# Second attention: sixteen slots for exponentials and another order of scores, products and maxima

## The chip, the core and the metric

The kernel runs on one core of one Trainium2 chip. The metric is the device time of one execution in microseconds (us), the median of the runs shown. TensorE is called PE, VectorE DVE, ScalarE ACT, GpSimd POOL and SyncE SP.

## The reference

Four batches of 1024 tokens of width 128 go through two layers, each of an attention and a feed-forward part, all with residuals and layer norms. Layer 0 is a causal attention with 16 heads of size 8 and then eight experts, of which each token takes two. Layer 1 is the attention that this change touches, and a feed-forward part with sines. Of the attention of layer 1, on `x_norm = rms_norm(x, g)`:

```python
q = (x_norm @ w_q).reshape(b, n, N_HEADS, D_HEAD)...   # 16 heads of 8
k = (x_norm @ w_k).reshape(b, n, KV_HEADS, D_HEAD)...  # 4 heads of keys and values
q = q * rf
k = k * rf
q5 = q.reshape(b, reps, KV_HEADS, n, D_HEAD)
qkt = jnp.einsum('brkqa,bkca->brkqc', q5, k) / scale
attn = jax.nn.softmax(qkt, axis=-1)                    # over all 1024 keys, no mask
s = jnp.einsum('brkqc,bkca->brkqa', attn, v)
o = s @ w_o
return s + o
```

## The kernel before

The program runs in stages that all engines pass in turn: projection and attention of layer 0 (with the routing of the experts laid between), the experts, projection of layer 1, attention of layer 1, feed-forward of layer 1. Semaphores tie the engines; each engine works through its own list in order.

An attention is done in **units**, one for a quad of four heads of one batch, 16 in all (`g` from 0). The softmax subtracts each row's maximum, so the scores are formed twice. In a unit of the second attention these are the steps; the letters are those of the string that gives their order:

- **a** (`pass_a`, L799, 32 in a unit): scores of 128 queries against all 1024 keys, two matmuls of 512 columns into one of two double banks of PSUM (banks 0 and 1, banks 2 and 3). DVE reduces them to the row maximum (L1481, 128x1024). A step a waits for the reduction of the a two before it. The a of unit g work for later units: a0 to a23 for heads 1 to 3 of unit g+1, a24 to a31 for head 0 of unit g+2. After a23's reduction DVE splits the 32 negated maxima into three bf16 parts (`negmax_split`, L1490 to L1494).
- **b** (`pass_b`, L832, 64 in a unit): transposed scores, 128 keys by 512 queries, with the maxima already subtracted through three more rows of the contraction; one matmul into one of three banks (4, 5, 7). It waits for the exponential of the b three before it, whose bank it takes. ACT then forms the exponential (L1221, 128x512) into a slot of `probs`.
- **p** (`pv`, L848, 16 in a unit): the product of four exponentials (the four heads j = 0 to 3 of one group m of 128 keys and half of the queries) with the values. Its four matmuls write 9 rows each at partitions 0, 32, 64 and 96 of bank 6; the data are float32, and the trace has two records for each matmul, eight for a p. The p of group m waits for the exponentials 4m to 4m+3. p0 to p7 make the first half of the queries, p8 to p15 the second.
- **c** (ACT, L1225): copy of a finished half out of bank 6, which the next half's first p waits for. **t** (`out_turn`, L864): four transposes of it into a bank that a step a would use. **n** (DVE, L1501 and L1506): division by the sums into `attn`.
- **m** (`negmax_turn`, L857): transpose of the split maxima of the next unit into a borrowed bank, and **s** (ACT, L1205) its copy, from which SP's DMA brings the maxima into Q for the next unit's b.

`c0` and `c1` and the like belong to the two halves. A t or m borrows the double bank of the step a that comes next, and that a waits for its reader (n or s); an m that uses the bank of a t waits for that t's n.

`ORDERS[1]` is the string. `Heads.order` turns it into a list of events, and PE, ACT and DVE each walk that list and do their own part of it, so the string sets the order on all three. Steps that a unit doesn't need are left out: unit 14 has no a24 to a31, unit 15 has no a, no m and no s. In unit 15 steps of the following feed-forward part are laid behind certain p (`EARLY`).

A slot of `probs` is used again after 8 exponentials: the first exponential of group m waits until p of group m-2 is done (`pv_done`, L1219 and L1220).

Of the kernel before, what the change touches and what calls it, by code (L numbers as in the profile page):

```python
# [25 lines left out]
P = 128  # L26
# [27 lines left out]
CROSS = SPL * SPL * HD  # L54
KROWS = CROSS + SPL
SLOTS = 4
PR = 8
HALF = 512

TWO_PI = 2.0 * np.pi  # L60
# [27 lines left out]
class Heads:  # L88
# [60 lines left out]

ORDERS = [  # L150
    "bbbbaabpaabbbabapabbbabbpbbbabapcabbbatbpnbababbabbapapaabbababbababbapbbbaabpbampsabbabbabbbappactn",
    "bbbbababbpbabbapbbababbpbabbabpbbababbpabbapbbababbpbbbapcabbtnbpbabbabbapbabbabbapabbbabpbbbababpmsbbbabapbabbbapapactn",
]


# [70 lines left out]
def build(nc, h_in, Wqvk, Wo0, router_w, gate_proj, up_proj, down_proj, w_q, w_k, w_v, w_o, g_rms,  # L226
# [9 lines left out]
    with ExitStack() as ctx:  # L236
        def sb(name, shape, dt=F32):
            return ctx.enter_context(nc.sbuf_tensor(name, shape, dt))
# [8 lines left out]
        Q = sb("Q", [P, SLOTS, 4, S], BF16)  # L247
        K = sb("K", [P, SLOTS, 4, S], BF16)
        V = sb("V", [P, SLOTS, 8, 4 * (HD + 1)])
        probs = sb("probs", [P, PR, HALF])  # L250
        oT = sb("oT", [P, HALF])
        rowmax = sb("rowmax", [P, 2, 32])
        negmax = sb("negmax", [P, SPL, 32], BF16)
# [32 lines left out]
        wg = sb("wg", [P, E, F0])  # L286
        wu = sb("wu", [P, E, F0])
# [87 lines left out]
        ps = ctx.enter_context(nc.psum_tensor("ps", [P, 8, 512], F32))  # L375

        def score_a(n):
            return ps[:, 2 * n:2 * n + 2, :].rearrange("p b n -> p (b n)")

        def turn_bank(unit):  # L380

            return 2 * (unit % 2)

        PV_BANK, B_BANKS = 6, (4, 5, 7)
# [350 lines left out]
        def _(pe):  # L735
# [47 lines left out]
            def attention(l):  # L783
                sl, hd = s[l], LAYERS[l]
                G, nB = hd.G, 4 * hd.G
                rows = HD + 1

                def pass_a(quad, slot, j, i):

                    n = 32 * quad + 8 * j + i  # L790
                    buf = score_a(i % 2)
                    kj = j if l == 0 else 0
                    if not isinstance(n, int) or n >= 2:
                        pe.wait_ge(sl["max_done"], n - 1)
                    w = hd.keys(i)
                    for c in range(0, w, 512):
                        e = min(c + 512, w)
                        diag = hd.causal and e == w
                        last = pe.matmul(buf[:, c:e], Q[0:CROSS, slot, j, i * P:(i + 1) * P],  # L799
                                         K[0:CROSS, slot, kj, c:e], start=True, stop=not diag)  # L800
                        if diag:
                            last = pe.matmul(buf[:, w - P:w], identb[:, :], causal[:, :],  # L802
                                             start=False, stop=True)
                    last.then_inc(sl["scores"], 1)
# [34 lines left out]
                def pv(g, q, m):  # L839
                    h, t = hd.groups[m]  # L840
                    c = hd.cols(m)
                    if t == 0:
                        pe.wait_ge(sl["o_copied"], 2 * g + h + AT_ONE)
                    for j in range(4):
                        n = nB * g + 4 * m + j
                        pe.wait_ge(sl["exp_done"], n + 4)
                        kj = j if l == 0 else 0
                        last = pe.matmul(ps[32 * j:32 * j + rows, PV_BANK, c:HALF],  # L848
                                         V[:, q, t, kj * rows:(kj + 1) * rows],
                                         probs[:, (4 * m + j) % PR, c:HALF],  # L850
                                         start=(t == 0), stop=(m == hd.last_of_half[h]), skip_group_check=True)
                    last.then_inc(sl["pv_done"], 1)

# [281 lines left out]
        def _(act):  # L1135
# [61 lines left out]
            def attention(l):  # L1197
                sl, hd = s[l], LAYERS[l]
                G, nB = hd.G, 4 * hd.G

                def negmax_copy(g, bank):
                    act.wait_ge(sl["negmaxT_psum"], g + 1)
                    if not isinstance(g, int) or g > 0:
                        act.wait_ge(sl["negmax_rows"], 16 * g)
                    act.activation(negmaxT[:, :], ps[0:SPL * 32, bank, 0:P // 2].bitcast(BF16),  # L1205
                                   ACT.Copy).then_inc(sl["negmaxT_ready"], 1)

                negmax_copy(0, turn_bank(1))

                def batch(b, final):  # L1210
                    for q in range(4):
                        g = 4 * b + q
                        for ev in hd.events:
                            if ev[0] == "B":
                                m, j = ev[1], ev[2]
                                n = nB * g + 4 * m + j
                                c = hd.cols(m)
                                act.wait_ge(sl["scoresT"], n + 1)
                                if j == 0:  # L1219
                                    act.wait_ge(sl["pv_done"], G * g + m + 1)  # L1220
                                act.activation(probs[:, (4 * m + j) % PR, c:HALF], ps[:, B_BANKS[(4 * m + j) % 3], c:HALF],  # L1221
                                               ACT.Exp, scale=SCALE).then_inc(sl["exp_done"], 1)
                            elif ev[0] == "OC":
                                act.wait_ge(sl["pv_done"], G * g + hd.last_of_half[ev[1]] + 3)
                                act.activation(oT[:, :], ps[:, PV_BANK, :], ACT.Copy)\  # L1225
                                    .then_inc(sl["o_copied"], 1)
                            elif ev[0] == "A" and l == 0:
                                route(0, 32 * g + ev[1])
                            elif ev[0] == "PV" and final and q == 3 and ev[1] in EARLY["scalar"][l]:
                                ff_prepare(*EARLY["scalar"][l][ev[1]], early=True)  # L1230
                            elif ev[0] == "MC" and not (final and q == 3):
                                negmax_copy(g + 1, turn_bank(ev[2]))

                for b in range(B - 1):
                    batch(b, False)
                batch(B - 1, True)

            def route(g, step):

                first = (1, 6)[g]  # L1240
                for kind, u in ROUTE["scalar"][g].get(step, ()):
                    if kind == "EX":
                        act.wait_ge(pre["small_read"], READS["SH", u] + 1)
                        if u >= 2:
                            act.wait_ge(pre["picked"], u - 1)
                        act.activation(exped[:, u % 2, :, :], shifted[:, u % 2, :, :], ACT.Exp).then_inc(pre["exped"], 1)
                        continue
                    act.wait_ge(pre["turned"], COPIES[kind, u] + 1)
                    if u >= 1:
                        before = {"CP1": "WO", "CP2": "LG"}[kind], u - 1  # L1250
                        act.wait_ge(pre["small"], SMALL[before] + 1)
                    act.activation((aT if kind == "CP1" else hT)[:, :], ps[:, first, :], ACT.Copy)\
                        .then_inc(pre["copied"], 1)
# [43 lines left out]
            def ff_prepare(u, stage, early=False):  # L1297
                first, third = (1, 1) if early else (0, 7)
                if stage == 0:
                    act.wait_ge(ff["a_turned"], u + 1 + AT_ONE)  # L1300
                    act.activation(aT[:, :], ps[:, first, :], ACT.Copy).then_inc(ff["a_ready"], 1)
                else:
                    act.wait_ge(ff["turned"], u + 1)
                    act.activation(hT_all[:, bass.ts(u, GW)], ps[:, third, :], ACT.Copy).then_inc(ff["h_ready"], 1)
# [53 lines left out]
        def _(dve):  # L1358
# [116 lines left out]
            def attention(l):  # L1475
                sl, hd = s[l], LAYERS[l]

                def row_max(quad, j, i, par):
                    n = 32 * quad + 8 * j + i
                    dve.wait_ge(sl["scores"], n + 1)  # L1480
                    dve.tensor_reduce(rowmax[:, par, 8 * j + i:8 * j + i + 1], score_a(i % 2)[:, 0:hd.keys(i)],  # L1481
                                      AX, ALU.max).then_inc(sl["max_done"], 1)
# [406 lines left out]
```

## Time and profile before

| | us |
|---|---|
| median of 3 runs | 1924.51 |
| lowest, highest | 1921.91, 1930.03 |
| the profiled execution | 1938.88 |
| its span, first to last instruction | 1937.0 |
| PE busy | 1737.0 (90%) |
| DVE busy | 1371.4 (71%) |
| ACT busy | 1133.1 (58%) |

The mean granted clock of TensorE is 0.943 of full speed. The second attention's unit 0 begins at about 1055 us of the span and its last transpose stands at 1818 us. Matmuls are pipelined: a row's length runs from a matmul's start to its modelled end and overlaps the next, so lengths of PE's work are better read from start to start. In the chain of work that ended last, PE has 70%, DVE 13%, ACT 5%.

### The profile page before, as it was taken

Reading aid. Unit: us, or ns where it says so; the run is one execution under the profiler, and the core shown is the slowest. Engines: PE = TensorE matmul, PEld = TensorE weight load, DVE = VectorE, ACT = ScalarE, POOL = GpSimd, SP = SyncE. Lnnn points to the kernel's source line nnn. Section 1 sums busy time; section 2 is a strip of 40 time slices with the busy share of each in tenths; the row PEclk is TensorE's granted clock in tenths of the full one; section 3 lists DMA queues with packets and bytes.
Section 4 is the critical chain, followed back from the end, with each engine's and each line's share of the span. In section 5 each row is a group of like instructions: output and inputs, shape, how many; then the busy total and the mean of one; then the engine's idle time right before and its main releaser. Section 6 shows DMA issues by size and latency. Waiting matters only on the chain.

```text
span 1937.0 us, 30817 instructions
## 1 busy us (share of the span) xinstructions
PE 1737.0 (90%) x10574; PEld 716.4 (37%) x10574; DVE 1371.4 (71%) x2373; ACT 1133.1 (58%) x2396; POOL 307.7 (16%) x407
## 2 busy tenths in 40 slices
PE   4599999998888898899868999999999999999886
PEld 2234444443333345565421222222222222222365
DVE  6577777777666625446598888888888888884386
ACT  3246666665444554233341777777777777777776
POOL 4100000002222124536440000000000000000265
PEclk9679999999888999999865999999999999999998
DMA  7645454432220011222242011111111111000000
GB/s 213 154 89 122 113 145 115 73 38 40 40 40 13 17 30 41 55 63 68 69 113 25 12 19 18 19 19 18 17 18 17 17 18 17 1 2 1 1 20 25
DMA packets 97576, 93.73 MB, mean 48 GB/s; under 512 B 47214, under 2 KB 75507, under 8 KB 95376
## 3 DMA queue, kind: packets, MB, share of 16 engines
q1 hardware_dynamic: 79872, 48.01, 15.5%
q0 software_dynamic: 9920, 37.87, 5.5%
q10 hardware_dynamic: 7632, 5.88, 1.1%
q8 instruction: 88, 1.44, 0.3%
q14 instruction: 64, 0.52, 0.1%
HBM read 48.03 MB, written 40.86 MB: 46 GB/s over the span
## 4 chain that ended last, share of the span: by engine, by line
PE 70%; DVE 13%; ACT 5%; issue 4%; POOL 3%; DMA 2%; ACTq 1%; another core or an unknown queue 1%; POOLq 0%; DVEq 0%; SPq 0%
PE ps L848 20%; PE ps L832 17%; PE ps L799 16%; DVE rowmax L1481 7%; PE ps L1028 3%; PE ps L1008 2%; PE ps L1000 2%; ACT probs L1221 2%; PE ps L864 2%; DMA k_parts<-Q 2%; PE ps L1018 2%; ACTq L1138 1%; PE ps L802 1%; PE ps L835 1%; PE ps L985 1%
## 5 line engine op out<-in xcount | busy, mean ns | idle before, releaser
L1481 DVE TENSOR_REDUCE rowmax<-ps 128x1 f32<-128x1024 f32 (+7 forms) x1024 | 974.9, 987 | 252.0 <-PE ps L802 123.2
L1221 ACT ACTIVATE probs<-ps 128x512 f32<-128x512 f32 (+3 forms) x1792 | 860.3, 556 | 386.0 <-PE ps L832 221.0
L799 PE MATMUL ps<-K,Q 72*128 72x512 bf16 (+3 forms) x1792 | 541.0, 376 | 55.9 <-DVE rowmax L1481 48.3
L832 PE MATMUL ps<-Q,K 75*128 75x512 bf16 (+3 forms) x1792 | 535.6, 361 | 14.7 <-ACT probs L1221 10.6
L848 PE MATMUL ps<-probs,V 128*9 128x512 f32 (+3 forms) x3584 | 445.2, 558 | 0.0
L832 PEld LDWEIGHTS ps<-Q,K 75*128 75x128 bf16 x1792 | 165.4, 98 | 371.9 <-ACT probs L1221 266.4
L799 PEld LDWEIGHTS ps<-K,Q 72*128 72x128 bf16 x1792 | 151.0, 99 | 357.5 <-DVE rowmax L1481 189.6
L580 POOL TENSOR_SCALAR rtmp<-mv 128x4 f32<-128x4 f32 x8 | 1.9, 232 | 806.1 <-DVE mv L1400 806.1
L1726 DVE TENSOR_TENSOR Q<-ps,Q 128x352 f32<-128x352 f32 x78 | 40.9, 524 | 114.2 <-ACT Q L1268 82.7
L802 PE MATMUL ps<-causal,identb 128*128 128x128 bf16 x512 | 116.6, 230 | 0.0
L848 PEld LDWEIGHTS ps<-probs,V 128*9 128x9 f32 x3584 | 60.7, 89 | 144.8 <-ACT probs L1221 76.8
L835 PE MATMUL ps<-identb,causal 128*128 128x128 bf16 x512 | 104.2, 222 | 0.0
L1277 ACT ACTIVATE Q<-ps,Q 128x128 f32<-128x128 f32 x78 | 28.6, 367 | 122.4 <-PE ps L1028 95.4
L620 POOL DMA_INDIRECT returned<-Q,target x78 | 78.0, 1000 | 120.9 <-ACT Q L1277 104.9
L591 POOL DMA_INDIRECT dispatch<-rows,index x64 | 62.3, 974 | 70.2 <-DVE rowmax L1481 32.2
L1028 PE MATMUL ps<-wd,Q 128*128 (+1 forms) x468 | 68.4, 284 | 3.6 <-issue 3.0
L1225 ACT ACTIVATE oT<-ps 128x512 f32<-128x512 f32 x64 | 38.4, 600 | 53.3 <-PE ps L848 53.3
L802 PEld LDWEIGHTS ps<-causal,identb 128*128 128x128 bf16 x512 | 51.9, 101 | 39.1 <-issue 5.5
L1008 PE MATMUL ps<-wu,Q 128*128 x156 | 64.0, 493 | 0.0
L1028 PEld LDWEIGHTS ps<-wd,Q 128*128 128x128 f32 (+1 forms) x468 | 60.4, 197 | 5.3 <-issue 4.7
L1000 PE MATMUL ps<-wg,Q 128*128 x156 | 61.5, 476 | 0.8 <-ACT Q L1260 0.8
L1501 DVE RECIPROCAL rden<-ps 128x16 f32<-128x16 f32 x64 | 16.0, 249 | 58.5 <-PE ps L864 58.3
(227 smaller groups left out, 1423.1 us busy)
## 6 DMA issues: line engine op xcount, KB each, us to landing
dispatch<-wg POOLq DMA_DIRECT2D x16, 1170.0 KB, 9.3
Q<-q_parts SPq DMA_DIRECT2D x288, 64.0 KB
K<-k_parts SPq DMA_DIRECT2D x144, 64.0 KB
q_parts<-Q POOLq DMA_DIRECT2D x16, 384.0 KB, 3.7
Q<-dispatch SPq DMA_DIRECT2D x78, 65.0 KB
probs<-returned SPq DMA_DIRECT2D x8, 512.0 KB, 4.0
k_parts<-Q POOLq DMA_DIRECT2D x8, 384.0 KB, 7.1
V<-v SPq DMA_DIRECT2D x16, 144.0 KB
```

The lines of the kernel that those rows point to most:

```text
L591: pool.indirect_dma_start(dispatch[u // GU][:, :], to, rows[:, u % 2, n // GT, n % GT, :], None)\
L620: pool.indirect_dma_start(returned[:, :], at, y_tile[:, k, :], None, bounds_check=2 * B * S - 1, oob_is_err=False).then_inc(tile_out[k], 16)
L799: last = pe.matmul(buf[:, c:e], Q[0:CROSS, slot, j, i * P:(i + 1) * P], K[0:CROSS, slot, kj, c:e], start=True, stop=not diag)
L802: last = pe.matmul(buf[:, w - P:w], identb[:, :], causal[:, :], start=False, stop=True)
L832: last = pe.matmul(ps[:, bank, c:HALF], K[0:KROWS, q, kj, t * P:(t + 1) * P], Q[0:KROWS, q, j, h * HALF + c:(h + 1) * HALF], start=True, s ...
L835: last = pe.matmul(ps[:, bank, c:c + P], causal[:, :], identb[:, :], start=False, stop=True)
L848: last = pe.matmul(ps[32 * j:32 * j + rows, PV_BANK, c:HALF], V[:, q, t, kj * rows:(kj + 1) * rows], probs[:, (4 * m + j) % PR, c:HALF], s ...
L1000: pe.matmul(ps[:, par, 0:F0], hT_tile[:, par, :], wg[:, bass.ds(expert, 1), :].rearrange("p a f -> p (a f)"), start=True, stop=True).then_ ...
L1008: pe.matmul(ps[:, 2 + par, 0:F0], hT_tile[:, par, :], wu[:, bass.ds(expert, 1), :].rearrange("p a f -> p (a f)"), start=True, stop=True).t ...
L1028: last = pe.matmul(ps[:, 5, P:2 * P], actsT[0:w, n % 2, c, :], wd[0:w, c, bass.ds(expert, 1), :].rearrange("p a d -> p (a d)"), start=(c = ...
L1221: act.activation(probs[:, (4 * m + j) % PR, c:HALF], ps[:, B_BANKS[(4 * m + j) % 3], c:HALF], ACT.Exp, scale=SCALE).then_inc(sl["exp_done" ...
L1481: dve.tensor_reduce(rowmax[:, par, 8 * j + i:8 * j + i + 1], score_a(i % 2)[:, 0:hd.keys(i)], AX, ALU.max).then_inc(sl["max_done"], 1)
```

## The change

The second attention gets 16 slots for exponentials. Slots 0 to 7 stay in `probs`; slots 8 to 11 lie on `wg` and 12 to 15 on `wu`, the gate and up weights of the experts. The first exponential of group m now waits for p of group m-4 (in the first unit the first four groups wait for none). The first attention keeps 8 slots and its order. The order string of the second attention is another one, with the same number of each letter.

```diff
-PR = 8
+PR = (8, 16)
...
 ORDERS = [
     "bbbbaabpaabbbabapabbbabbpbbbabapcabbbatbpnbababbabbapapaabbababbababbapbbbaabpbampsabbabbabbbappactn",
-    "bbbbababbpbabbapbbababbpbabbabpbbababbpabbapbbababbpbbbapcabbtnbpbabbabbapbabbabbapabbbabpbbbababpmsbbbabapbabbbapapactn",
+    "bbbbaabbpbabbabbbabbabpbabbabpbababbpbbaabbpbbababpbbababpbabbabpcbababpbabbabpbababbpabbbtpnmsbbbaabbpbabbapbbbaappactn",
 ]
...
-        probs = sb("probs", [P, PR, HALF])
+        probs = sb("probs", [P, PR[0], HALF])
...
+        def prob(l, n):
+
+            k = n % PR[l]
+            if k < PR[0]:
+                return probs[:, k, :]
+            room = (wg, wu)[(k - PR[0]) // 4]
+            return room[:, :, :].rearrange("p e f -> p (e f)")[:, (k % 4) * HALF:(k % 4 + 1) * HALF]
...
-                                         probs[:, (4 * m + j) % PR, c:HALF],
+                                         prob(l, 4 * m + j)[:, c:HALF],
...
-                                if j == 0:
-                                    act.wait_ge(sl["pv_done"], G * g + m + 1)
-                                act.activation(probs[:, (4 * m + j) % PR, c:HALF], ps[:, B_BANKS[(4 * m + j) % 3], c:HALF],
+                                if j == 0 and (l == 0 or G * g + m >= PR[1] // 4):
+                                    act.wait_ge(sl["pv_done"], G * g + m + 3 - PR[l] // 4)
+                                act.activation(prob(l, 4 * m + j)[:, c:HALF], ps[:, B_BANKS[(4 * m + j) % 3], c:HALF],
```

Counted along the two strings, this many b have been issued at each p, and this many a:

```
p        0   1   2   3   4   5   6   7   8   9  10  11  12  13  14  15
before
 b       7  10  15  19  24  26  31  34  37  42  47  51  56  60  64  64
 a       2   4   6   8  10  12  14  15  16  19  22  24  26  28  30  31
after
 b       6  15  19  23  27  31  35  39  42  46  50  53  58  61  64  64
 a       2   6   8  10  12  14  16  18  20  22  24  25  27  29  31  31
```

The step t0 stood between b35 and b36 and n0 behind it; now t0 stands before p11, and n0, m and s behind p11. Before, m stood behind p12.

## Rows read from the trace of the kernel before

**Rows 1.** The page's slices: PE's busy share in tenths, 40 equal slices.
```profile
PE   4599999998888898899868999999999999999886
```

**Rows 2.** Windows: units 1 to 13, unit 14, unit 15; busy us, instructions.
```profile
core 0: us, PE busy (x) PEld busy (x) DVE busy (x) ACT busy (x) POOL busy (x), PEclk, DMA share, GB/s
...
1106.10:1725.50 619.40, 612.03 (x3447) 176.77 (x3446) 512.09 (x521) 455.41 (x871) 0.00 (x0) 1.00 0.12 16
1725.50:1771.80 46.30, 44.27 (x252) 12.72 (x251) 30.44 (x33) 34.92 (x67) 0.00 (x0) 1.00 0.01 2
1771.80:1818.90 47.10, 41.98 (x246) 13.54 (x243) 7.88 (x32) 35.39 (x69) 2.42 (x4) 1.00 0.00 1
```

**Rows 3.** Waits of ACT in units 1 to 13: total us, times, longest.
```profile
ACT probs L1221 <- PE ps L832: 126.9, 169, 1.4
```

**Rows 4.** Timeline, start of unit 5: start, length, engine, work, [idle before].
```profile
1296.71 0.81 PE L832 MATMUL ps<-Q,K 75*128 75x512 bf16 x3
1297.13 3.54 ACT L1221 ACTIVATE probs<-ps 128x512 f32<-128x512 f32 x7 [1.03 <-PE ps L832]
...
1297.78 0.39 PE L832 MATMUL ps<-Q,K 75*128 75x512 bf16 x1 [0.26 <-ACT probs L1221]
...
1298.00 0.60 PE L799 MATMUL ps<-K,Q 72*128 72x512 bf16 x2
...
1298.64 2.36 DVE L1481 TENSOR_REDUCE rowmax<-ps 128x1 f32<-128x1024 f32 x2 [0.92 <-PE ps L799]
...
1301.69 0.60 PE L799 MATMUL ps<-K,Q 72*128 72x512 bf16 x2
...
1302.21 1.05 PE L848 MATMUL ps<-probs,V 128*9 128x512 f32 x8
...
1303.19 0.60 PE L832 MATMUL ps<-Q,K 75*128 75x512 bf16 x2
```

**Rows 5.** Timeline, middle of unit 5: p8, n0, then a18.
```profile
1321.31 1.38 PE L848 MATMUL ps<-probs,V 128*9 128x512 f32 x8
...
1321.44 0.25 DVE L1501 RECIPROCAL rden<-ps 128x16 f32<-128x16 f32 x1
...
1321.73 0.29 DVE L1506 TENSOR_TENSOR attn<-ps,rden 128x128 f32<-128x128 f32 x1
...
1324.15 0.59 PE L832 MATMUL ps<-Q,K 75*128 75x512 bf16 x2
...
1324.76 0.61 PE L799 MATMUL ps<-K,Q 72*128 72x512 bf16 x2
```

**Rows 6.** Timeline of DVE: five reductions, end of the split.
```profile
1327.14 5.79 DVE L1481 TENSOR_REDUCE rowmax<-ps 128x1 f32<-128x1024 f32 x5 [0.17 <-PE ps L799]
...
1333.62 0.19 DVE L1494 TENSOR_TENSOR negmax<-negrest,negmax 128x32 bf16<-128x32 f32 x1
```

**Rows 7.** Timeline, end of unit 5: a31, the copy, t1, unit 6's b.
```profile
1343.01 0.60 PE L799 MATMUL ps<-K,Q 72*128 72x512 bf16 x2
1343.15 0.60 ACT L1225 ACTIVATE oT<-ps 128x512 f32<-128x512 f32 x1 [1.81 <-PE ps L848]
...
1343.89 0.63 PE L864 MATMUL ps<-ident,oT 128*128 128x128 f32 x4 [0.27 <-ACT oT L1225]
...
1344.35 0.81 PE L832 MATMUL ps<-Q,K 75*128 75x512 bf16 x3
```

**Rows 8.** Timeline of PE, end of unit 14; the last row is p15.
```profile
1766.98 0.82 PE L832 MATMUL ps<-Q,K 75*128 75x512 bf16 x3
...
1768.38 2.17 PE L848 MATMUL ps<-probs,V 128*9 128x512 f32 x16
...
1769.24 1.31 PE L848 MATMUL ps<-probs,V 128*9 128x512 f32 x8
```

**Rows 9.** Timeline of PE, unit 15: p7, a feed-forward step, p8.
```profile
1793.82 1.35 PE L848 MATMUL ps<-probs,V 128*9 128x512 f32 x8
...
1795.71 0.63 PE L739 MATMUL ps<-ident,tokens 128*128 128x128 f32 x4 [0.53 <-ACT Q L1304]
...
1797.36 1.40 PE L848 MATMUL ps<-probs,V 128*9 128x512 f32 x8
```

## The prediction

> **What bounds the kernel now.** I read the slices first: the second attention is the long plateau before the end, PE at 9 tenths [rows 1]. The windows cut it up: thirteen whole units (a unit is one quad of heads of one batch) in 619.4 us, PE busy 612.0 of them at granted clock 1.00, DVE 512, ACT 455; then unit 14, without its last eight a, and unit 15, with none [rows 2]. So TensorE sets the pace, and another order pays only by what it takes out between PE's instructions. These gaps I took from the starts of PE's rows. Unit 5 begins at 1296.71, unit 6 at 1344.35: 47.64 us [rows 4, 7]. About 1.6 us of this is standing still, in five places:
> - the fourth b of a unit: three b fill the three score banks, the fourth starts at 1297.78, 0.42 us after its turn, when the first exponential has ended [rows 4];
> - p8 lasts 1.38 us where p1 lasts 1.05: its last exponential comes from b35, with one b between, so 0.33 us [rows 4, 5];
> - a18 and a21: two b start at 1324.15 and the next a at 1324.76, 0.61 later, where two b take 0.44; this a waits for a reduction on DVE. Twice 0.18 [rows 5];
> - t1, at the end: the a before it starts at 1343.01, t1 at 1343.89, 0.44 after its turn, since ACT's copy (1343.15, 0.60 us) must end first [rows 7].
> The rest is stream: a b 0.22 us, an a (two matmuls) 0.44; p1 to the next b 0.98 (1302.21 to 1303.19), and 0.09 more to get into p (the a at 1301.69 and p1 are 0.52 apart) [rows 4]; t 0.46 [rows 7].
> No exponential waits for a slot: in the thirteen units L1221 waits for scores (L832) alone [rows 3]. Eight slots don't hold ACT; they only forbid another order.
>
> **Slots.** Slots 8 to 15 lie on weights that the experts read last. The same instructions write and read the same shapes there; none is added. The wait of an exponential goes from two groups back to four. When p of group k is issued, the b ahead of it reach at most group k+2, which waits for p of group k-2, long done: 0 us. Attention one keeps eight slots and its order: 0 us. Of other queues only SP is touched: its DMA of the negated maxima follows m, which comes earlier in the unit: 0 us.
>
> **Order, what goes.** six b now stand between b35 and p8: 0.33 gone. For the a I went through the unit and set each against the reduction two before it (a reduction starts 0.64 after its a, 1298.00 to 1298.64, and five of them last 5.79 us, the last 1.22, so 1.14 apart [rows 4, 6]): none is late, the two 0.18 go. p14 and p15 become neighbours. The trace has that pair in unit 14, where the a between them is left out: p14 at 1768.38, p15 at 1769.24, 0.86 apart, against 0.98+0.09 = 1.07 [rows 4, 8]: 0.20 gone. Together 0.33+0.36+0.20 = 0.89 us a unit.
>
> **Order, what is new: the first stretch.** Between p0 and p1 there are now 9 b and 4 a (were 3 and 2). PE's stream there is 9 x 0.22 + 4 x 0.44 = 3.7 us; ACT needs 9 x 0.49 = 4.4 (seven exponentials in 3.54 us, one 0.60, so 0.49 apart [rows 4]). Walked through from the unit's start: p0 at 2.69, b6 3.67, b7 4.32, b8 4.54, b10 5.41, b11 due at 5.63. An exponential starts 0.42 after its b (1296.71 to 1297.13 [rows 4]) unless one is before it: the sixth at 4.09, then 4.74, 5.22, ending 5.81; b11 takes the bank of the eighth and starts at 5.86: stop 0.23. In the same way b13, due at 6.74, waits for the tenth until 6.84: 0.10. After it come few b for long (b14, p1, b15, a6): no more stops. I take 0.33; bounds 0 and 0.7, by which ACT's sum exceeds PE's.
>
> **Order, what is new: t0, p11, n0, m.** Before, m stood five p after n0. Now PE does t0, p11 and then m in the same bank, which n0 (DVE) must first have read, and n0 stands on DVE behind a23's reduction, the split of the maxima and a24's reduction. The fifth reduction of the row ends at 1332.93, so starts at 1331.71, and the split ends at 1333.81, 2.1 us later [rows 6]. In the new order, from a22's start: reductions of a22 and a23 at 0.64 and 1.78, split over at 3.88, a24's reduction at about 3.9, reciprocal 1.14 later at 5.04, n0's product over 0.58 after that (1321.44 to 1322.02 [rows 5]) at 5.62, m from 5.68. PE would be at m after a22, b, a23 (1.09), two b (0.44), p10 (1.07), a24 (0.44), three b (0.66), t0 (0.46), p11 (1.07) = 5.23. Stop 0.45. Bounds: 0, if DVE is through earlier, and 0.45+1.14, if one more reduction stands before n0. I take 0.45. Three b follow m; ACT's copy, for which a25 waits, falls inside them. DVE has some 8 us spare in a unit (512 of 619), so it catches up.
> What it costs to get from t0 into p11 no row shows, as a b or an a stands before every p. I count 0.09 as elsewhere; bounds 0 and 0.31, the whole step from b to p.
> The Trainium skill ("TensorEngine Tiling (Array Packing)", Key Properties) says that a change of the tiling mode drains the engine. By this, t0 (the whole array) to p11 (four strips of columns) pays as b to p does, and the sum stands; if getting into p were a matter of the data type, t0 being float32 as p is, it would cost nothing and the sum would be 14 x 0.09 = 1.3 us lower. The trace agrees so far as p14 to p15 shows neither an entry nor an exit.
> New stops 0.33+0.45 = 0.78, so **units 0 to 13: -0.89+0.78 = -0.11 us each, -1.5 together.** The stops at the fourth b and at t1 stay.
>
> **Unit 14.** p8 and two a -0.69, first stretch +0.33, no stop at m (no a24, so n0 is done before p11 ends). Where no a stands between, three b go at once after a p and the fourth waits for the first exponential: 1766.98 to 1768.38 is 1.40 for four b and the entry [rows 8]; three cost 0.75, a fifth 0.49 more. The groups before p12, p13, p14 were 5, 4, 4 (4.7 us), now 5, 3, 3 (3.4), the two missing b standing earlier at 0.22 each: -0.85. p15 follows sooner on the last b, so its wait for the last exponential (1.31 long against 1.05: 0.26 [rows 4, 8]) grows to 0.4. Sum -1.0.
> **Unit 15.** The b before p0 to p15 come as 7, 3, 5, 4, 5, 2, 5, 3, 3, 5, 5, 4, 5, 4, 4, 0, now as 6, 9, 4, 4, 4, 4, 4, 4, 3, 4, 4, 3, 5, 3, 3, 0. By the same prices 22.8 against 22.5 us, -0.3. p8 (1.40 long [rows 9]) -0.35. After p7 PE stands 0.91 (1793.82+0.98 to 1795.71 [rows 9]) for an ACT copy, now about 0.7. p15 +0.15. Sum -0.7. The feed-forward steps hang on the numbers of p and keep their order.
> Total -1.5-1.0-0.7 = -3.2 us: the profiled execution from 1938.88 to 1935.7 us (its span from 1937.0 to 1933.8). The median stands 14.4 us below that execution, so 1924.5-3.2 = **1921 us**.
>
> **Rivals.**
> Faster: the two new stops don't come (exponentials closer together than 0.49, DVE through sooner). Then 0.89 x 14 + 2 = 14 us less, 1910. For it: both are differences of 0.1 to 0.5 us between sums of five. Against: DVE's rows show no slack between reductions that follow each other.
> Slower: m waits for a whole reduction more than I count, because a24's reads late or n0 finds one in front. That is 1.14 a unit, +16 us, 1937; it gets over 0.5% once n0 is 0.9 us later than counted. Against it: a25 comes after m on PE, so only a24's own delay can do it. A pitch of ACT above 0.55 in the first stretch has the same sign, +0.5 a unit, 1928.
> The change doesn't do what it says: the slots are no gain by themselves. My forecast holds that already; the rival is that the order gains nothing either, within 2 us of 1924.5.
>
> **How the numbers follow.** What a measurement can tell from no change is 0.5%, 9.6 us. Forecast 0.65, no gain 0.13, faster rival 0.13, slower rival 0.09. Both outer rivals are partly inside 0.5%, and the tails of the forecast reach out: faster (below 1914.9) 0.14, within 0.79, slower (above 1934.1) 0.07. The range takes new stops of 0.3 to 1.4 us a unit, 1912 to 1930.
>
> **What would show it.** Right: unit length near 47.5; p8 1.05 long; every a on its turn; p14 to p15 0.86; 0.2 to 0.3 lost at b11 and about 0.45 before m, with n0's product ending just ahead of m; unit 14 near 45.3 us. Wrong: no gap before m (faster), one above 1 us (slower), gaps at other b or a, or a clock under 1.00 inside the units.

## The result, and the profile after

| us | before | after |
|---|---|---|
| median of 5 runs each, side by side | 1921.91 | 1911.92 |
| lowest, highest | 1921.6, 1930.03 | 1910.65, 1916.67 |
| the profiled execution | 1938.88 | 1916.67 |
| its span | 1937.0 | 1914.8 |
| mean granted clock | 0.943 | 0.942 |

The ratio is 0.9945, with a 95% interval of 0.9921 to 0.997: 0.55% faster. The forecast was 1921 with a range of 1912 to 1930, so it was wrong: the time lies just below the range. The direction of the small forecast gain was right, its size was not. The profiled execution of after is the slowest of its five; that of before is slower than any of its five. Of the 87 executions of before measured beside the runs below, one took 2438.21 us at a mean granted clock of 0.64 and is left out of the ratios.

Where does the time go? First the slices of PE after the change, which answer to [rows 1], then three windows that answer to [rows 2]: units 1 to 13 from the first b of unit 1, then unit 14 and unit 15. Columns are start and end, length, busy time and instructions of PE, its weight loads, DVE, ACT and POOL, the granted clock, the DMA share and GB/s.
```profile
PE   4599999999888889999878999999999999999876
```
```profile
1089.40:1706.10 616.70, 604.24 (x3448) 182.97 (x3446) 510.25 (x521) 463.74 (x871) 0.00 (x0) 1.00 0.12 16
1706.10:1751.20 45.10, 43.60 (x251) 12.71 (x249) 30.45 (x33) 35.52 (x67) 0.00 (x0) 1.00 0.01 2
1751.20:1798.00 46.80, 41.17 (x246) 13.28 (x244) 7.97 (x33) 35.28 (x69) 2.43 (x4) 1.00 0.00 1
```
The plateau and its bound are as before. A whole unit takes 616.7 / 13 = 47.44 us against 619.4 / 13 = 47.65, so 0.21 less where 0.11 was forecast. The other units, by their first b in both traces: unit 0 50.35 (before 50.8), unit 14 45.1 (46.3), unit 15 up to t1 45.9 (46.6). From the first b of the second attention to its last transpose it is 758.5 us against 763.5. That is **5.0 us found in the place that the change touches**, where 3.2 was forecast. Units 1 to 14 have these lengths within 0.02 us in each other trace of the two kernels (again_before, again_after and after_3, below), which makes 3.8 of the 5.0; units 0 and 15 differ from execution to execution.

The two spans differ by 22.2 us, though. Cut into stages, 19 us of these lie in the experts, whose work the change leaves alone: 235.9 us before, 216.8 after, from DVE's first step there (L1726, in after L1734) to its last. Two windows of equal place show it (before, then after; PE's granted clock is the third number from the end), and under them the row of before's DVE that stands idle there:
```profile
760.00:775.00 15.00, 11.36 (x53) 7.50 (x52) 4.93 (x19) 3.23 (x11) 8.40 (x12) 0.77 0.15 44
...
768.07 0.53 DVE L1726 TENSOR_TENSOR Q<-ps,Q 128x352 f32<-128x352 f32 x1 [6.31 <-issue]
```
```profile
760.00:775.00 15.00, 15.00 (x88) 9.88 (x87) 8.14 (x28) 5.37 (x16) 10.83 (x15) 1.00 0.25 68
```
In before, PE, DVE and ACT halt together, and the profile names only "issue" or "remote" as what they wait for. It was one execution's mishap: a copy of before, below, has 216.1 us in this stage. So neither difference of whole executions can be read as the change's; its own trace must be read unit by unit.

**The new stops of a unit**, in unit 5 of after. It answers to [rows 4]: the first three b, the first exponential, the fourth b; then the b before b11, and b11.
```profile
1279.12 0.81 PE L840 MATMUL ps<-Q,K 75*128 75x512 bf16 x3
...
1280.19 0.39 PE L840 MATMUL ps<-Q,K 75*128 75x512 bf16 x1 [0.26 <-ACT probs L1229]
...
1284.32 1.08 PE L840 MATMUL ps<-Q,K 75*128 75x512 bf16 x3
1285.23 0.60 PE L807 MATMUL ps<-K,Q 72*128 72x512 bf16 x2
1285.67 0.71 PE L840 MATMUL ps<-Q,K 75*128 75x512 bf16 x2
```
The fourth b still starts 0.42 after its turn. The first row of three b (b9 to b11) takes 0.91 from 1284.32 to the next a at 1285.23, where three b at 0.22 take 0.66: the stop of 0.25 sits before its last b, forecast 0.23. The pair after it takes 0.54 instead of 0.44: the 0.10 of b13, as forecast.

The middle, answering to [rows 5, 6]: p8, then t0, p11 and m with DVE's steps between.
```profile
1306.46 1.05 PE L856 MATMUL ps<-probs,V 128*9 128x512 f32 x8
...
1307.44 0.39 PE L840 MATMUL ps<-Q,K 75*128 75x512 bf16 x1
...
1314.17 0.60 PE L872 MATMUL ps<-ident,oT 128*128 128x128 f32 x4
1314.28 1.22 DVE L1489 TENSOR_REDUCE rowmax<-ps 128x1 f32<-128x1024 f32 x1
1314.70 1.05 PE L856 MATMUL ps<-wu,V 128*9 128x512 f32 x8
...
1315.70 0.29 DVE L1514 TENSOR_TENSOR attn<-ps,rden 128x128 f32<-128x128 f32 x1
...
1316.09 0.23 PE L865 MATMUL ps<-identb,negmax 128*96 128x128 bf16 x1 [0.34 <-issue]
```
p8 is 0.98 long from start to start, its 0.33 gone. p11 starts at 1314.70, and what follows a p starts 0.98 later; n0's product on DVE ends at 1315.99, and m starts at 1316.09, where it would have started at 1315.68. The stop is 0.41. The profile calls it "issue", but the end of n0 0.1 before m names what it waited for.

The end, answering to [rows 7, 8]: p14, p15, the last a, t1 and unit 6's first b.
```profile
1323.39 1.05 PE L856 MATMUL ps<-wg,V 128*9 128x512 f32 x8
1324.25 1.04 PE L856 MATMUL ps<-wu,V 128*9 128x512 f32 x8
1325.23 0.60 PE L807 MATMUL ps<-K,Q 72*128 72x512 bf16 x2
...
1326.10 0.63 PE L872 MATMUL ps<-ident,oT 128*128 128x128 f32 x4 [0.27 <-ACT oT L1233]
...
1326.57 0.60 PE L840 MATMUL ps<-Q,K 75*128 75x512 bf16 x2
```
p14 to p15 is 0.86, and t1 still waits 0.43. In units 14 and 15 the smaller terms came too: from p15 to t1 2.25 and 2.24 (before 2.09 in both), p8 of unit 15 0.98 (before 1.33), its p7 to the next step 2.19 (before 2.35).

### The profile page after: what moved, and what is told of

Same layout as the page of the kernel before. It is cut to its first block, busy times and chain, and to the rows that moved or that the text cites. A ratio compares the mean times of both kernels' runs of the same rounds, so it can differ in the third digit from the quotient of the medians.

```text
span 1914.8 us, 30798 instructions
## 1 busy us (share of the span) xinstructions
PE 1728.9 (90%) x10574; PEld 720.4 (38%) x10574; DVE 1369.1 (72%) x2373; ACT 1142.7 (60%) x2396; POOL 308.7 (16%) x407
## 4 chain that ended last, share of the span: by engine, by line
PE 68%; DVE 14%; ACT 5%; issue 4%; POOL 3%; DMA 3%; ACTq 1%; POOLq 0%; DVEq 0%; SPq 0%
PE ps L856 20%; PE ps L840 17%; PE ps L807 16%; DVE rowmax L1489 7%; PE ps L1036 2%; PE ps L1016 2%; PE ps L1008 2%; DMA k_parts<-Q 2%; ACT probs L1229 2%; PE ps L872 2%; PE ps L1026 2%; ACTq L1146 1%; PE ps L810 1%; PE ps L843 1%; ACT oT L1233 1%
## 5 line engine op out<-in xcount | busy, mean ns | idle before, releaser
L1229 ACT ACTIVATE probs<-ps 128x512 f32<-128x512 f32 (+3 forms) x1280 | 601.1, 535 | 295.6 <-PE ps L843 157.5
L807 PE MATMUL ps<-K,Q 72*128 72x512 bf16 (+3 forms) x1792 | 530.8, 376 | 52.8 <-DVE rowmax L1489 46.0
L840 PE MATMUL ps<-Q,K 75*128 75x512 bf16 (+3 forms) x1792 | 547.1, 361 | 15.3 <-ACT probs L1229 8.4
L840 PEld LDWEIGHTS ps<-Q,K 75*128 75x128 bf16 x1792 | 166.1, 98 | 388.2 <-ACT probs L1229 157.7
L856 PE MATMUL ps<-probs,V 128*9 128x512 f32 (+3 forms) x2560 | 305.2, 543 | 0.0
L807 PEld LDWEIGHTS ps<-K,Q 72*128 72x128 bf16 x1792 | 157.0, 99 | 320.7 <-DVE rowmax L1489 140.8
L1229 ACT ACTIVATE wu<-ps 128x512 f32<-128x512 f32 x256 | 142.0, 608 | 43.0 <-PE ps L840 42.1
L1229 ACT ACTIVATE wg<-ps 128x512 f32<-128x512 f32 x256 | 143.7, 601 | 29.0 <-PE ps L840 27.1
L1734 DVE TENSOR_TENSOR Q<-ps,Q 128x352 f32<-128x352 f32 x78 | 40.8, 524 | 98.8 <-ACT Q L1276 84.7
L856 PEld LDWEIGHTS ps<-probs,V 128*9 128x9 f32 x2560 | 43.1, 89 | 94.5 <-issue 44.2
L856 PE MATMUL ps<-wu,V 128*9 128x512 f32 x512 | 67.8, 594 | 0.0
L856 PE MATMUL ps<-wg,V 128*9 128x512 f32 x512 | 67.0, 595 | 0.0
```

Of the source, the lines that this page charges most:

```text
L840: last = pe.matmul(ps[:, bank, c:HALF], K[0:KROWS, q, kj, t * P:(t + 1) * P], Q[0:KROWS, q, j, h * HALF + c:(h + 1) * HALF], start=True, s ...
L1229: act.activation(prob(l, 4 * m + j)[:, c:HALF], ps[:, B_BANKS[(4 * m + j) % 3], c:HALF], ACT.Exp, scale=SCALE).then_inc(sl["exp_done"], 1)
L1734: dve.tensor_tensor(acts[:, par, 0:F0], ps[:, 2 + par, 0:F0], gated[:, par, :], ALU.mult)\
```

## Experiments

Ten runs, each measured beside a run of before in the same turn. The first four share one set of before (median 1922.17, n 29), m_late, lead3_8slots and no_pair another (1920.51), the last three a third (1921.22). Each of these kernels was run 12 times, order_8slots 6 times. The ratios are not exactly the quotients of the medians given (for ramp 1.0018 against 1.0028).

**again_before** is before with no edit.

> The kernel before, run again beside itself, for what an execution varies by. Theory A (the 5 us that the second attention doesn't explain are chance of the executions, mostly in the experts stage, which took 235.9 us in the profile of before and 216.8 us in that of after, with the same instructions): ratio to before 1.000 within 0.3%, second attention 763.5 us within 0.5, unit 47.65, but an experts stage that differs from 235.9 us, likely near 217. Theory B (the change shortens the stages outside the second attention too): experts stage again near 236 us.

Measured: 1921.91, ratio 0.9995 (0.998 to 1.0011), unit 47.65, experts 216.1 us, span 1923.0. What follows: the 19 us do not belong to the kernel before; they are one execution's. The same program ran from 1912.8 to 1929.3 in those 29 runs, and the 1924.51 of three runs lay 2.3 above their median.

**again_after** and, in the last turn, **after_3** are the changed kernel with no edit.

> The changed kernel again, on the same chip as its control. Theory A: second attention 758.5 us within 0.5, unit 47.44, and a time 5 to 6 us below the control (ratio 0.997). Theory B: again 10 us below (ratio 0.9945), with an experts stage near 217 us while the control has 236.

> The changed kernel a third time. Chance outside the second attention: 5 us below before, as its units say, within the interval (ratio 0.9974). Change acts elsewhere too: 7 to 10 us below, with an interval that leaves 5 out.

Measured: again_after 1914.46, ratio 0.9962 (0.9946 to 0.9977); after_3 1916.62, ratio 0.9969 (0.9956 to 0.9981). Units are 47.44 in both. 5.0 us of 1922 is 0.26%, ratio 0.9974: inside the intervals of again_after and after_3, and outside that of the first five runs. By the medians after is 7.7 and 4.6 us below the before beside it. The gain is real and of 5 to 8 us; of the first 10 a part was most likely chance.

How single executions come to differ shows in again_after's unit 15, 2.9 us longer than after's with the same instructions. Ten us from 1.2 us after the unit's first b, in again_after and then in after:
```profile
1751.00:1761.00 10.00, 9.81 (x31) 2.00 (x31) 0.00 (x0) 6.81 (x14) 0.00 (x0) 0.53 0.01 2
```
```profile
1752.40:1762.40 10.00, 8.78 (x44) 2.21 (x43) 0.00 (x0) 8.75 (x19) 0.00 (x0) 1.00 0.01 2
```
At a granted clock of 0.53 (near the lower of its two levels, 1.2 GHz) PE gets 31 instructions done in the time of 44. Nothing in the program differs. The clock also falls in unit 15 of after_3 and m_late (mean granted clock 0.96, 1.3 and 1.4 us longer) and of order_8slots (0.81), and not in m_late_2, no_pair or ramp, nor in the three traces with the order of before.

**slots_only**: sixteen slots, the order string of before.
```diff
 ORDERS = [
...
-    "bbbbaabbpbabbabbbabbabpbabbabpbababbpbbaabbpbbababpbbababpbabbabpcbababpbabbabpbababbpabbbtpnmsbbbaabbpbabbapbbbaappactn",
+    "bbbbababbpbabbapbbababbpbabbabpbbababbpbabbapbbababbpbbbapcabbtnbpbabbabbapbabbabbapabbbabpbbbababpmsbbbabapbabbbapapactn",
```

> Sixteen slots with the order of before. Theory 'order' (no exponential waited for a slot, so slots alone are worth nothing): unit 47.65 us, second attention 763.5 us, ratio 1.000. Rival 'slots' (writing and reading other addresses or the longer wait distance is itself worth time): unit at or near 47.44 us and 3 to 5 us less.

Measured: 1921.2, ratio 0.9999 (0.9982 to 1.0016). The first b of units 5 and 6:
```profile
1281.38 0.81 PE L840 MATMUL ps<-Q,K 75*128 75x512 bf16 x3
...
1329.02 0.81 PE L840 MATMUL ps<-Q,K 75*128 75x512 bf16 x3
```
47.64 apart, as before. The slots alone bring nothing, and laying them over the experts' weights costs nothing.

**order_8slots**: the new order with eight slots.
```diff
-PR = (8, 16)
+PR = (8, 8)
```

> The new order with eight slots (the first exponential of group m waits for p of group m-2). Theory 'the lead needs the slots': with seven b ahead, the first exponential of group k+2 must wait for p of group k, so ACT starts it about 1.1 us after p's start, and the b three places on waits for it: some 0.3 to 0.8 us lost at most p, unit 52 to 58 us, 80 to 160 us slower in all. Rival 'slots are idle here': p ends early enough, unit within 1 us of 47.44.

Measured: 2076.24, ratio 1.0836 (1.0789 to 1.0882), unit 56.50, second attention 913.9 us. The timeline shows a p, the four exponentials behind it and the b behind these:
```profile
1333.84 1.05 PE L856 MATMUL ps<-probs,V 128*9 128x512 f32 x8
...
1335.02 2.06 ACT L1229 ACTIVATE probs<-ps 128x512 f32<-128x512 f32 x4 [1.71 <-PE ps L856]
...
1335.67 0.39 PE L840 MATMUL ps<-Q,K 75*128 75x512 bf16 x1 [0.78 <-ACT probs L1229]
```
ACT stood 1.71 us for the p, then PE 0.78 for ACT. The waits of ACT between 1089 and 1706 us (sum, times, longest) say the same of the whole stretch. In order_8slots:
```profile
ACT probs L1229 <- PE ps L856: 203.3, 140, 1.9
...
ACT probs L1229 <- PE ps L840: 17.2, 23, 1.2
```
In after the exponentials wait for scores (L840) alone:
```profile
ACT probs L1229 <- PE ps L840: 52.5, 78, 1.0
ACT wu L1229 <- PE ps L840: 34.1, 52, 0.9
...
ACT wg L1229 <- PE ps L840: 23.1, 52, 0.7
```
So this order needs the slots, and the slots are worth nothing without it: the two parts are one change.

**m_late** and, again, **m_late_2**: m and s go one p later, so n0 is done before PE is there; the p between has other neighbours.
```diff
-    "bbbbaabbpbabbabbbabbabpbabbabpbababbpbbaabbpbbababpbbababpbabbabpcbababpbabbabpbababbpabbbtpnmsbbbaabbpbabbapbbbaappactn",
+    "bbbbaabbpbabbabbbabbabpbabbabpbababbpbbaabbpbbababpbbababpbabbabpcbababpbabbabpbababbpabbbtpnbbbaabbpmsbbbaapbbbaappactn",
```

> The changed kernel with m and s put behind p12 again, where they stood before; t0, p11 and n0 stay. Theory (m stands 0.41 us a unit because n0 comes behind a24's reduction): the gap between p11 and m goes, unit 47.44-0.41 = 47.03 us, second attention 5 to 6 us shorter than the 758.5 of the changed kernel, near 753, and the time about 11 us below before. Rival (the wait only moves: a25 must wait for n0 anyway, or a27 for ACT's copy of m's result): unit 47.3 to 47.5.

> m_late once more, beside the changed kernel and ramp. If times outside the second attention are chance: unit 47.09, and 10 us below before as its units say (14 x 0.56, and 2.3 in units 0, 14 and 15), within the interval. If the change also acts elsewhere: 13 us or more below.

Measured: m_late 1911.07, ratio 0.9957 (0.9938 to 0.9976); m_late_2 1913.83, ratio 0.9965 (0.9949 to 0.998). Unit 47.09, 0.35 less than after's. The stop is gone: the b follows p11 after 0.99, and m follows p12 after 0.98, as anything does.
```profile
1312.39 1.05 PE L856 MATMUL ps<-wu,V 128*9 128x512 f32 x8
1313.38 0.82 PE L840 MATMUL ps<-Q,K 75*128 75x512 bf16 x3
...
1315.42 1.05 PE L856 MATMUL ps<-probs,V 128*9 128x512 f32 x8
1316.40 0.26 PE L865 MATMUL ps<-identb,negmax 128*96 128x128 bf16 x1
```
The second attention takes 755.3 and 753.6 us here, and 758.5, 761.9 and 759.5 in the three traces of after, 763.5 and 765.9 in the two of before. By the units this is the best version seen; by the medians it can't be told from after, as the intervals overlap.

**lead3_8slots** (its edit is against before): is a lead over three groups needed at all? Eight slots, no group more than eight exponentials ahead, p8 still clear of its last exponential, m late, p14 and p15 apart.
```diff
PR = 8
...
+    "bbbbababbpbabbapbbababbpbabbabpbababbpbbaabbpbbababpbbababpcbabbabpbababpbabbabpbababbpabbbtpnbbbaabbpmsbbbaapbbbaapactn",
```

> Eight slots, and an order that has the first four p of before (7, 10, 15, 19 b issued), then the groups of the changed one shifted by one p, so that three b and not seven stand ahead; m behind p13; p14 and p15 apart. Theory (the depth of slots is worth nothing, the stops are all): no stop at b11 and b13 (-0.35), none at m (-0.41), the pair p14, p15 gone (+0.20): unit 46.9 us, second attention near 751, 12 to 13 us below before. Rival (the lead of seven itself saves time, through exponentials that are always ready): stops of 0.1 to 0.4 us come back at several p and the unit is at 47.3 or above.

Measured: 1922.01, ratio 1.0011 (0.9994 to 1.0028), unit 47.65: a miss by 0.75 us a unit. Two products, p12 and p15, behind b's that stand close to them show why:
```profile
1315.74 1.40 PE L848 MATMUL ps<-probs,V 128*9 128x512 f32 x8
1317.08 0.82 PE L832 MATMUL ps<-Q,K 75*128 75x512 bf16 x3
...
1324.43 1.44 PE L848 MATMUL ps<-probs,V 128*9 128x512 f32 x8
1325.80 0.39 PE L799 MATMUL ps<-K,Q 72*128 72x512 bf16 x1
```
1.34 and 1.37 from p to the next instruction instead of 0.98: the last exponential of the b just ahead isn't ready, 0.36 and 0.39 lost. Together they are 0.75, the whole miss. In this order a stop cured at p8 comes back at p12, which has one b and t0 between it and the last b that it needs, and at p15, which has two a. In the new order six b stand between the two at p12, and the whole of p14 at p15, and neither stops: the lead does pay, which the expectation had put at nothing.

**no_pair**: after's order with the last a between p14 and p15 again.
```diff
-    "bbbbaabbpbabbabbbabbabpbabbabpbababbpbbaabbpbbababpbbababpbabbabpcbababpbabbabpbababbpabbbtpnmsbbbaabbpbabbapbbbaappactn",
+    "bbbbaabbpbabbabbbabbabpbabbabpbababbpbbaabbpbbababpbbababpbabbabpcbababpbabbabpbababbpabbbtpnmsbbbaabbpbabbapbbbapapactn",
```

> The changed kernel with a30 between p14 and p15 again. Theory (a pair of p saves one exit and one entry): unit 47.44+0.20 = 47.64 us. Rival (the 0.86 between p14 and p15 is paid back at the last copy and t1, which wait for p15): unit 47.44.

Measured: 1920.42, ratio 0.9987 (0.9969 to 1.0004), unit 47.67, 0.23 more than after's. The step that was 0.86 is now p14, a, p15:
```profile
1323.95 1.05 PE L856 MATMUL ps<-wg,V 128*9 128x512 f32 x8
1324.93 0.60 PE L807 MATMUL ps<-K,Q 72*128 72x512 bf16 x2
1325.46 1.05 PE L856 MATMUL ps<-wu,V 128*9 128x512 f32 x8
```
1.51 for a p and an a, which by stream take 0.86 + 0.44 = 1.30. So 0.21 a unit is what the neighbours save, as forecast (0.20). And 47.67 is before's 47.65: without this pair, all the rest of the change comes to nothing in a unit, since the new stops pay back what the old ones gave. No run has the pair with eight slots and before's order otherwise, so whether it needs the slots at all is not shown.

**ramp**: sixteen slots, the b spread so that the first stretch, p12 and p15 have room, and m late.
```diff
+    "bbbbababbpbabbapbbababbpbabbabbpbabbabbpbabbabbpbabbabbpbabbabpcbababpbabbabpbababbpabbbtpnbbbaabbpbabbapmsbbbaapaapactn",
```

> Sixteen slots; the lead is built up in steps of one (7, 10, 15, 20, 25, 30, 35, 39 b issued at p0 to p7) and not in one stretch of nine b; t0 before p11, m behind p13, a30 and a31 around p15, no pair. Theory (the first stretch stops because ACT gets nine exponentials in 3.7 us of PE's work; a lead of five or more covers a p that follows t0 or the last b): no stop but those at the fourth b and at t1, so 47.09 of m_late -0.35 +0.20: unit 46.95 us, 10 us or more below before. Rival (the stops at p12 and p15 of lead3_8slots had another cause than the short lead): they stay, unit 47.6.

Measured: 1926.69, ratio 1.0018 (1.0002 to 1.0034), unit 48.06: a miss by 1.1 us a unit, with the wrong sign. The stops it was written against are gone, but now two steps a wait for DVE, a26 and a30:
```profile
1328.28 0.59 PE L840 MATMUL ps<-Q,K 75*128 75x512 bf16 x2
...
1329.18 0.60 PE L807 MATMUL ps<-K,Q 72*128 72x512 bf16 x2 [0.31 <-DVE rowmax L1489]
...
1327.79 0.19 DVE L1502 TENSOR_TENSOR negmax<-negrest,negmax 128x32 bf16<-128x32 f32 x1
1327.90 3.48 DVE L1489 TENSOR_REDUCE rowmax<-ps 128x1 f32<-128x1024 f32 x3
1332.07 4.62 DVE L1489 TENSOR_REDUCE rowmax<-ps 128x1 f32<-128x1024 f32 x4 [0.68 <-PE ps L807]
...
1333.37 0.61 PE L807 MATMUL ps<-K,Q 72*128 72x512 bf16 x2
...
1334.48 0.60 PE L807 MATMUL ps<-K,Q 72*128 72x512 bf16 x2 [0.50 <-DVE rowmax L1489]
```
DVE takes one maximum each 1.14 us, and PE brings the a faster than that: stops of 0.47 and 0.67, together the whole miss. At the first, the split of the maxima also stands on DVE before the reduction that is waited for (a24's, from 1327.90); at the second it is the bunch of a27 to a30 alone. The average (in after, DVE busy 510 of the 617 us of units 1 to 13) hides this; a bunch of a is bound by DVE.

## Why the prediction was wrong

**Mechanism: right.** Each term that the forecast gave for the second attention is in the trace, at its place. The last four rows are sums:

| term, us | forecast | measured |
|---|---|---|
| p8 | -0.33 | gone (0.98 long) |
| a18, a21 | -0.36 | gone, every a on its turn |
| p14 and p15 neighbours | -0.20 | -0.21 (no_pair +0.23) |
| stops at b11, b13 | +0.33 | +0.35 |
| stop at m | +0.45 | +0.41 (m_late -0.35) |
| a whole unit | -0.11 | -0.21 |
| unit 14 | -1.0 | -1.1 |
| unit 15 | -0.7 | -0.7 |
| second attention | -3.2 | -5.0 |

The 0.10 a unit between forecast and trace is the stop at m, 0.04 less, those at b11 and b13, 0.02 more, and some 0.08 of small steps that no term covered. Over units 1 to 13 it makes 1.3 us, and unit 14 gives 0.1. The remaining 0.34 comes from unit 0, and it can't be given to the change: unit 0 took 50.0 to 54.4 us in the traces of all kernels but order_8slots, by when the clock rises in it (granted 0.52 in one stretch of again_before).

**The rival that m waits for a whole reduction** (1937) is out: n0 was 0.1 ahead of m and never a reduction late. **The rival without new stops** (1910) is out too, although the time came close to it: both stops stand in the trace at 0.35 and 0.41. Whoever saw only the time would have taken the wrong one. **That the order gains nothing** is out as well, by 0.21 a unit, though the slots alone gain nothing, as the forecast held.

**The term no row of before showed**, from t0 into p11: the last transpose and p11 start 0.20 apart, where transposes follow each other by 0.11. So 0.09 was paid, as by a b or an a that goes over into a p, though both are float32 here. That speaks for the drain on a change of tiling mode that the Trainium skill names ("TensorEngine Tiling (Array Packing)", Key Properties), against a price for the data type.
```profile
1314.50 0.27 PE L872 MATMUL ps<-ident,oT 128*128 128x128 f32 x1
1314.70 0.62 PE L856 MATMUL ps<-wu,V 128*9 128x512 f32 x4
```
The whole step from t0 to p11 is 0.53, against the 0.46 + 0.09 counted.

**The step that failed is the last one**: "The median stands 14.4 us below that execution, so 1924.5-3.2". It was off in two terms. First, 3.2 for the second attention was 5.0. Second, 1924.5 was taken as the fixed time of before; it was the median of three runs of a program that runs from 1912.8 to 1929.3, with a median of 1922.2 over 29 (1921.91 in the five runs of the result). 1922.2-5.0 = 1917.2, and after's medians of 12 are 1914.46 and 1916.62. The 2.5 to 4.7 us from these down to 1911.92, the median of the first five, did not come back and were most likely chance; what lies between 1917.2 and these medians stays open, as said below. The range failed with it: its ends took "new stops of 0.3 to 1.4 us a unit" alone, the unknown costs, and left nothing for the base. Its sum is off too: by the forecast's own terms stops of 0.3 give 1924.5-1.7-14 x 0.59 = 1914.5, and its 1912 would want stops of 0.12. The chance of 0.14 on faster failed too: 9.6 us below 1924.5 is only 7.3 below 1922.2.

**Open**: the three comparisons of after say -0.55, -0.38 and -0.31%, the trace -0.26%. All lie to the same side. Whether some 2 us of a real gain stand outside the second attention can't be told from these runs. The one stage that leans this way is what comes before the experts: the last transpose of the first attention stands at 704.1 and 706.0 us in the two traces of before, and at 704.0, 703.2 and 702.5 in those of after; but ramp has it at 708.4, so single executions differ by more.

## What to carry to other kernels

More buffers are worth what the order that they permit is worth: read whether anything waits for a slot now, and if nothing does, price only the order. Ask of each part of the order what it brings by itself: here the net gain of a unit is as large as that of two neighbouring products alone. In a pipeline of three engines, move one step past each engine's own pitch (here 0.49 for an exponential, 1.14 for a reduction) and walk the sum of starts through the unit; a stop moved to a bunch elsewhere takes back the gain, as ramp and lead3_8slots did. And give a base measured in three runs a width of its own before adding a difference that is smaller.

## What the runs showed of the hardware

- Two float32 products p (four matmuls each, of 512 columns, with 9 rows out at partitions 0, 32, 64 and 96) follow each other in 0.86 us (after, p14 to p15); with a bf16 a of 0.44 between them they take 1.51 (no_pair), 0.21 more than both; getting from a float32 transpose over the whole array into one costs 0.09 (after, t0 to p11).
- The granted clock can fall to about half in unit 15 in one execution and not in the next of the same program: 0.53 over 10 us in again_after, against 1.00 in after, 2.9 us. PE had been about as busy before in both: 12.59 of the 14 us to 1751 in again_after, 11.99 of the 13.4 us to 1752.4 in after. No cause is shown.
- One execution of before lost 19 us in the experts with PE, DVE and ACT idle together; in the eleven other traces of these kernels the stage took 215.9 to 218.5 us. No cause is shown.
